# Cross-attention and gated FFN on one core: TensorE's matmuls in another order by forms of tiles

## The reference, cut to what matters

```python
q = layernorm(x) @ Wq + bq;  k = ctx @ Wk + bk;  v = ctx @ Wv + bv
scores = einsum('bhqd,bkd->bhqk', q, k) / sqrt(16)
scores = where(mask == 0, -1e9, scores)
x = x + (softmax(scores) @ v).reshape(b, s, 256) @ Wo + bo          # "x1"
xm = mix(layernorm(x))                     # three neighbouring tokens, weighted
idx = argmax(tanh(xm @ Wo1 + bo1) @ Wo2 + bo2)                      # one of nine paths
y = (xm @ W1[idx] + b1[idx]) @ W2[idx] + b2[idx]
out = x + layernorm(layernorm(x) + y) * gamma + beta
```

## Time and profile before

| | before |
|---|---|
| median of 3 runs | 337.5 us (337.3, 337.5, 338.87) |
| profiled execution | 338.19 us, its span 336.4 us |
| PE busy | 304.2 us, 90% of the span |
| DVE busy | 263.4 us, 78% |
| POOL busy | 218.2 us, 65% |
| ACT busy | 183.3 us, 54% |
| mean granted TensorE clock | 0.977 |

### The profile page before, as it was taken

One profiled execution on the slowest core, in us unless ns is written; L12 is line 12 of the kernel. 1 busy time (PEld: TensorE's weight loads), 2 busy tenths in 40 slices (PEclk: granted clock), 3 DMA queues, 4 the chain that ended last, 5 costly groups with the idle time before them and its releaser, 6 DMA issues. The chain is left out here.

```text
span 336.4 us, 7161 instructions
## 1 busy us (share of the span) xinstructions
PE 304.2 (90%) x2764; PEld 229.7 (68%) x2764; DVE 263.4 (78%) x610; ACT 183.3 (54%) x284; POOL 218.2 (65%) x259
## 2 busy tenths in 40 slices
PE   1687889699899999999999999999999999899991
PEld 1574366376567967796678767796779677876891
DVE  1776698998569796989879796989399768495876
ACT  1353906705883576727871778457653655356620
POOL 0192331892097579984996499957886598519454
PEclk9999779959999999999999999999999999999998
DMA  7932020002002001200111001000100010001003
GB/s 216 249 81 79 2 78 3 0 3 78 3 0 80 2 0 64 62 19 3 62 32 50 0 20 47 1 2 0 64 2 1 3 64 0 0 2 50 14 3 125
DMA packets 20587, 13.16 MB, mean 39 GB/s; under 512 B 10113, under 2 KB 20426, under 8 KB 20554
## 3 DMA queue, kind: packets, MB, share of 16 engines
q1 hardware_dynamic: 18914, 12.14, 12.5%
q10 hardware_dynamic: 1640, 0.57, 0.8%
HBM read 8.51 MB, written 4.19 MB: 38 GB/s over the span
## 5 line engine op out<-in xcount | busy, mean ns | idle before, releaser
L1519 POOL TENSOR_TENSOR rs<-ve,halfneg 128x4 f32<-128x4 f32 x22 | 23.6, 1072 | 49.6 <-DVE ve L1164 49.6
L905 ACT ACTIVATE e<-ps 128x1024 f32<-128x1024 f32 x32 | 31.1, 1024 | 14.1 <-PE ps L584 14.1
L1201 DVE TENSOR_REDUCE mx<-ps 128x16 f32<-128x1024 f32 x32 | 38.0, 1215 | 0.3 <-PE ps L547 0.3
L1612 POOL TENSOR_TENSOR hml<-hs,hmh 128x512 fp32r<-128x512 f32 x28 | 35.0, 1280 | 4.6 <-ACT hmh L967 4.6
L707 PE MATMUL ps<-w2h,hmh 128*128 128x256 f32 (+1 forms) x140 | 35.1, 288 | 0.0
L620 PE MATMUL ps<-wo,osb 128*128 128x256 f32 x128 | 34.1, 416 | 0.2 <-DVE osb L1228 0.2
L708 PE MATMUL ps<-w2l,hmh 128*128 128x256 f32 (+1 forms) x140 | 34.1, 280 | 0.0
L1321 DVE TENSOR_TENSOR hs<-hs,ps 128x512 f32<-128x512 f32 x28 | 18.6, 684 | 17.3 <-PE ps L687 17.3
L1577 POOL TENSOR_TENSOR y<-xh2f,gms 128x256 f32<-128x256 f32 x24 | 20.4, 882 | 16.2 <-DVE xh2f L1173 16.2
L930 ACT ACTIVATE xh<-x,vb,rs 128x256 f32<-128x256 f32 x24 | 12.5, 591 | 31.5 <-POOL vb L1532 31.5
L620 PEld LDWEIGHTS ps<-wo,osb 128*128 128x128 f32 x128 | 25.2, 206 | 5.4 <-issue 0.4
(11 more groups left out here) (174 smaller groups left out, 800.6 us busy)
## 6 DMA issues: line engine op xcount, KB each, us to landing
xin<-in_x SPq DMA_DIRECT2D x8, 512.0 KB, 3.9
out<-y SPq DMA_DIRECT2D x6, 512.0 KB, 2.9
min_<-in_mask_Bx1xSxS_ik SPq DMA_DIRECT2D x8, 128.0 KB, 3.9
hs<-in_L_ffn_W SPq DMA_DIRECT2D x2, 288.0 KB
hs<-in_L_ffn_W SPq DMA_DIRECT2D x1, 512.0 KB
out<-y SPq DMA_DIRECT2D x2, 256.0 KB, 2.1
out<-xin SPq DMA_DIRECT2D x2, 256.0 KB, 2.3
cst<-in_constants SPq DMA_DIRECT2D x1, 384.0 KB, 6.8
```

The source lines that it names most:

```text
L905: nc.scalar.activation(e[:, 2 * i:2 * i + 2, :], ps[:, bank:bank + 2, :], ACT.Exp).then_inc(s_e, 1)
L1201: v.tensor_reduce(mx[:, k, :].rearrange("p (a h) -> p a h", a=2), ps[:, bank:bank + 2, :].rearrange("p a (h s) -> p a h s", s=SK), AX.X, A ...
L1519: g.tensor_tensor(ln[7][:, :], ln[6][:, :], halfneg[:, :], ALU.pow).then_inc(s_r, 1)
L1612: g.tensor_tensor(L.lo(m, r), L.selected(m, r), L.hi(m, r).bitcast(F32), ALU.subtract).then_inc(L.s_hl, 1)
```

## The change

Three things move; no instruction is added or taken away.

1. In `scores_transposed` the groups' banks change: groups 0 and 2 take banks 2 and 3, groups 1 and 3 take 4 and 5, and the exponential writes its two groups to e with a stride. L572's matmuls go in the order 0, 2, 1, 3. The maximum's pass (32*128) goes ahead of the mask's (64*128), which is now last and carries `s_st`. The wait for `s_nT` now stands ahead of both.
2. In PE's step with an f: rep 1 and rep 2 follow each other, then the two `scores_for_max` 0 and 1; rep 3 and rep 4 follow each other, and `scores_for_max` 2 goes behind `project_out` (2, 3), beside number 3.
3. In DVE's step with an f, `take_max` 2 goes behind both `x1_stats`, beside number 3.

```diff
+        PAIR_ORDER = (0, 2, 1, 3)
+        SCORE_BANK = [2 + PAIR_ORDER.index(g) for g in range(4)]
...
+                for g in PAIR_ORDER:
+                    if t and g < 2:
+                        pe.wait_ge(s_e, at(b, NJ * 4, j * 4 + g + 1))
+                    nc.tensor.matmul(ps[:, SCORE_BANK[g], :], ksth[quarter(g), :], qr[quarter(g), t, :], start=True, stop=False)
                 for g in range(4):
-                    if t and g % 2 == 0:
-                        pe.wait_ge(s_e, at(b, NJ * 4, j * 4 + g // 2 + 1))
-                    nc.tensor.matmul(ps[:, 2 + g, :], ksth[quarter(g), :], qr[quarter(g), t, :], start=True, stop=False)
...
-                for g in (0, 2, 1, 3):
-                    r = half_rows(g // 2)
-                    nc.tensor.matmul(ps[:, 2 + g, :], mask_ident[r, 0:P], mT[r, j, :], start=False, stop=False)
                 if t == 0:
                     pe.wait_ge(s_nT, at(b, NJ, j + 1))
                 for g in range(4):
-                    nc.tensor.matmul(ps[:, 2 + g, :], max_rows[quarter(g), t * P:(t + 1) * P], nmT[quarter(g), :],
+                    nc.tensor.matmul(ps[:, SCORE_BANK[g], :], max_rows[quarter(g), t * P:(t + 1) * P], nmT[quarter(g), :],
+                                     start=False, stop=False)
+                for g in PAIR_ORDER:
+                    r = half_rows(g // 2)
+                    nc.tensor.matmul(ps[:, SCORE_BANK[g], :], mask_ident[r, 0:P], mT[r, j, :],
                                      start=False, stop=True).then_inc(s_st, 1)
...
                 if f:
                     rep(*f, 1)
+                    rep(*f, 2)
                     if front:
                         scores_for_max(*front, 0, banks)
-                    rep(*f, 2)
-                    if front:
                         scores_for_max(*front, 1, banks)
...
                     rep(*f, 3)
-                    if front:
-                        scores_for_max(*front, 2, banks)
                     rep(*f, 4)
                 if n:
                     project_out(*n, (2, 3))
                 if f and front:
+                    scores_for_max(*front, 2, banks)
                     scores_for_max(*front, 3, banks)
...
-                    bank = 2 + 2 * (i % 2)
-                    nc.scalar.activation(e[:, 2 * i:2 * i + 2, :], ps[:, bank:bank + 2, :], ACT.Exp).then_inc(s_e, 1)
+                    g = i % 2
+                    nc.scalar.activation(e[:, 4 * half + g:4 * half + g + 3:2, :], ps[:, 2 + 2 * g:4 + 2 * g, :],
+                                         ACT.Exp).then_inc(s_e, 1)
...
-                    if front:
-                        take_max(*front, 2, banks)
                     if n:
                         x1_stats(*n, 0)
                         x1_stats(*n, 1)
                     if front:
+                        take_max(*front, 2, banks)
                         take_max(*front, 3, banks)
                         split_max(*front)
```

More of the change, by code:

```diff
@@ L568, in scores_transposed @@
                     pe.wait_ge(s_mx, at(b, NJ * NT, (j + 1) * NT))
+                for g in PAIR_ORDER:
+                    if t and g < 2:
+                        pe.wait_ge(s_e, at(b, NJ * 4, j * 4 + g + 1))
+                    nc.tensor.matmul(ps[:, SCORE_BANK[g], :], ksth[quarter(g), :], qr[quarter(g), t, :], start=True, stop=False)
                 for g in range(4):
-                    if t and g % 2 == 0:
-                        pe.wait_ge(s_e, at(b, NJ * 4, j * 4 + g // 2 + 1))
-                    nc.tensor.matmul(ps[:, 2 + g, :], ksth[quarter(g), :], qr[quarter(g), t, :], start=True, stop=False)
-                for g in range(4):
-                    nc.tensor.matmul(ps[:, 2 + g, :], kstl[quarter(g), :], qr[quarter(g), t, :], start=False, stop=False)
+                    nc.tensor.matmul(ps[:, SCORE_BANK[g], :], kstl[quarter(g), :], qr[quarter(g), t, :], start=False, stop=False)
                 pe.wait_ge(s_ql, at(b, NJ * KD, j * KD + t + 1))
                 for g in range(4):
-                    nc.tensor.matmul(ps[:, 2 + g, :], ksth[quarter(g), :], ql[quarter(g), t, :], start=False, stop=False)
-                for g in (0, 2, 1, 3):
-                    r = half_rows(g // 2)
-                    nc.tensor.matmul(ps[:, 2 + g, :], mask_ident[r, 0:P], mT[r, j, :], start=False, stop=False)
+                    nc.tensor.matmul(ps[:, SCORE_BANK[g], :], ksth[quarter(g), :], ql[quarter(g), t, :], start=False, stop=False)
                 if t == 0:
```

## The result

| | before | after |
|---|---|---|
| median of 16 runs each, side by side | 337.62 us (336.14 to 340.15) | 335.67 us (334.14 to 338.67) |
| profiled execution, and its span | 338.19 us, 336.4 us | 336.16 us, 334.4 us |
| mean granted clock | 0.977 | 0.974 |

The ratio is 0.9942, 95% interval [0.9919, 0.9964]: 2.0 us faster, where 3.3 us were forecast. The time lies in the range (332.3 to 336.1), 1.5 us above the forecast of 334.2. Lines have moved by two to four: L574, L577, L584, L580 of before are now L577, L580, L584 (maxima) and L588 (mask); L543 is L545, L612 L616, L620 L624, L687 L691, L707 L711, L1217 L1220, L905 L907.

The account below looks back on a forecast made before the run. PE's order was taken as the bound between 84 and 262 us, with DVE nearly so before. Terms 2.25 + 0 + 1.05 = 3.3 us off the profiled 338.19 us, adjusted to the runs' median, gave 334.2 us, range 332.3 to 336.1.

Parts of the forecast that it names:

- A change of form costs about 0.1 us: PE's matmul passes: switching tile form costs about 0.1 us at full clock; scores were to save 0.09 us at 16 places.
- the change doesn't do what it says: Rival: the 0.1 us belongs to the two-round pass or returns in a longer first pass; 337.3 us, chance 0.09.
- the weighed rule's sum of 3.6 us: Skill's rule that tiling-mode changes drain the engine: 36 changes at 0.1 us give 3.6 us, plus what earlier exponentials bring.
- The first pair is swallowed by the wait for osb: One-hots and score tiles, first four: second tile still waits for DVE's normalised attention, so the saving is 0 us.
- Earlier exponentials: ACT starts 0.3 us earlier behind the mask's first round; with scores' savings 0.57 us in (0,0), 0.39 in (0,1) and (1,0).
- The two passes of scores give 0.09 for t = 0: Step (0,1): 0.09 us from the scores at t = 0, with 0.3 for the earlier release, makes 0.39 us.
- 0.39 us by the same sum: Step (1,0): PE's 0.91 us wait for ACT's hidden 0, behind the exponential, shortens by 0.39 us.
- DVE passes the gain on: Steps (0,0) and (0,1): DVE's reciprocal waits for PE, 1.8 us in all, so PE's earlier arrival is not lost there.
- 2 x 0.09 us each are left: Five steps (1,1) to (3,1): PE doesn't wait for the exponential, so only the scores' saving remains, 0.9 us together.
- It is cover for later and no gain: DVE's moved reduction: statistics come 1.2 us sooner, but PE's t2 doesn't wait for them in these steps; 0 us.
- the first steps keep their time: Rival: before 84 us DVE or the clock eats the gain, and rep 2's wait bites; 335.7 us, chance 0.18.
- The rival of the spared clock: Rival: the earlier exponential spares the low-clock stretch in the projection of (0,1), 1.9 us; 332.3 us, chance 0.08.

Follow-up runs that it names:

- E2: Kernel before with the new order of PE's and DVE's steps (one-hots, score tiles, reduction), its scores as they were: median 335.72 us, ratio 0.9974.
- E6: Changed kernel with rep 2 back between score tiles 0 and 1: a single run, 337.43 us.
- E3: Changed kernel with the groups in their old banks and both exponentials of a half released by the mask's last matmul: median 335.01 us, ratio 0.9936.
- E10: Changed kernel with seven useless matmuls where PE waits for DVE's inverse in (0,0) and (0,1): median 334.79 us, ratio 0.9894.
- E11: Kernel before with the same seven useless matmuls in (0,0) and (0,1), on the same chip as E10: median 336.97 us, ratio 0.9965.
- the filled pair: E10 and E11, the changed kernel and the kernel before, each with seven useless matmuls at PE's waits: 2.2 us apart by median.
- E5: Changed kernel with take_max 2 back in its old place in DVE's step, PE's order as changed: median 338.91 us, ratio 1.0017.
- E4: Changed kernel with seven useless matmuls where PE waits for DVE's inverse in (0,0) and (0,1), an earlier run: median 334.2 us, ratio 0.9908.

## Why the prediction was right, and where it was too large

The direction and the range held, and so did the sign of each part but for (0,1) and (3,1); the sum was 1.3 us too large. By its own steps:

- **A change of form costs about 0.1 us**: right. The scores give 0.10 us for each pass set (0.09 forecast), rep 3 to W2 0.22 (0.21), and E2 gives 0.20 to 0.21 us in each of four steps. The rival that the change doesn't do what it says is out. So is the weighed rule's sum of 3.6 us: E6 shows that the changes of form in the first four bring nothing where a wait stands behind them, and the rest was partly lost.
- **The first pair is swallowed by the wait for osb**: right, by E6. Rep 2's wait for ACT came, and the room behind it fell to 0.08 us in odd steps, but it doesn't bite: the second score tile stays 1.47 us behind rep 1.
- **Earlier exponentials**: the mechanism was right (the exponential of (0,0) starts at 30.73 and not 31.04, the waits are 0.99, 0.91 and 0.69 us and not 1.20, 1.12 and 0.91, and E3 takes this back). But ACT's wait of 0.27 us in (0,0), taken as a second saving, is a term that failed: that wait exists only when the scores before it fall in a low stretch. In this pair they did, and PE led by 45.92 - 45.20 = 0.72 us at the projection; then the projection, reached sooner, had more of its matmuls in the next low stretch, 4.84 us against 4.49, and the lead at the end of the step was 0.36. At the full clock (E10, E11), counted from the step's first pass, the lead is 0.30 at both places. So the low clock first gave and then took, and what (0,0) lacks of the 0.57 is that term.
- **"The two passes of scores give 0.09 for t = 0" in (0,1), and "0.39 us by the same sum" in (1,0)**: the release came, the 0.09 us did not. The product behind these scores waits for its transposed input, and PE gets there no sooner. From the first scores of t = 0 to those of t = 1 both kernels take 5.63 to 5.64 us in either step (52.36 to 57.99 in before, 52.00 to 57.64 in after), and in (1,0) of E11 and then of E10 the wait takes up what was saved, PE's timeline:

```profile
78.87 0.73 PE L449 MATMUL ps<-xTh,wqh 128*128 128x512 f32 x2 [0.69 <-DVE xTl L1195]
```

```profile
78.38 0.73 PE L451 MATMUL ps<-xTh,wqh 128*128 128x512 f32 x2 [0.78 <-DVE xTl L1198]
```

- **"DVE passes the gain on"**: this is the step that failed in (0,1). DVE's reciprocal did start 0.65 us sooner (64.16 against 64.81), but the cast behind it went from 0.32 to 0.58 us, and PE's lead fell from 0.66 to 0.39 us. The low clock took 0.20 us more, and the forecast -0.39 became +0.16; in the filled pair it is -0.05.
- **"2 x 0.09 us each are left" in (1,1) to (3,1)**: true in even steps, half true in odd ones, where the cast reaches 0.45 us and the spread starts at 135.08 and not at about 134.99, 0.55 behind the row at 134.44. In (3,1) nothing was left: PE's wait for rDs went from 0.2 to 0.4 us.
- **"It is cover for later and no gain"**: right for the difference as forecast, wrong as a reading of the change. E5 shows that without DVE's move PE's order loses 0.64 us in a middle step. I had costed DVE's move against the old place of PE's tile, and not against the new one, where DVE would stand 1.05 us waiting for it.
- **(1,0)** gave 0.49 of 0.60 us (0.54 in the filled pair). The step's order gave its 0.21 (E2); the missing 0.1 us is the 0.09 for t = 0, as told above.

The shortfall by steps in the plain pair: 0.21 us in (0,0), 0.55 in (0,1), 0.11 in (1,0), 0.21 in the four steps behind it and 0.22 from (3,1) on, which is 1.30 us, the 3.3 forecast less the 2.0 measured. In the filled pair on one chip the gain is 2.2 us, so only about 0.2 of the 1.3 is the clock's. The rest is in terms of the sum: 0.27 in (0,0) for ACT's second wait, about 0.26 in (0,1) for the cast, 0.09 each in (0,1) and (1,0) for t = 0, 0.2 in the odd steps for the cast, and 0.2 to 0.3 from (3,1) on, where the last part differs by 0.1 us and more between runs of the same code and can't be divided further. Of the rivals, "the first steps keep their time" comes nearest in time (335.7 us) and in place: (0,0) and (0,1) together gave 0.20 of 0.96 us. Its second cause, rep 2's wait, came but cost nothing.

The rival of the spared clock did not come by itself. E4 and E10, which are one kernel, show what it is worth: their medians are 1.5 and 0.9 us below the changed kernel's 335.67, measured at other times, and 3.2 and 3.6 us below that of the kernel before measured beside them. That is the fastest kernel of this study.

## What to carry to other kernels

Where one engine is the bound, read its timeline by starts and put neighbours of one tile form together: each change of form saved was 0.1 us, but only where no wait stands behind it. When an engine arrives sooner, look at what the engine that it feeds runs beside: here a lead of 0.66 us was cut to 0.39 where an operation of a third engine, for which nobody waited, was under way. A wait seen in one profile is a saving only if it would be there without the low clock: the 0.27 us of ACT's were not. And if a tile is moved on the producer, move its reader by the same distance, or the reader's queue stands still in front of it.

## What the runs showed of the hardware that I had not expected

- The low stretches of the clock (the 1.2 GHz level) came at the same times in before and after, though PE stood 0.7 us apart: a lead that runs into such a stretch is cut (4.84 against 4.49 us for the same 16 matmuls). In other runs they lay elsewhere (E3: 22.2 to 25.6 and 66.5 to 73.4 us). With seven useless matmuls in each of two waits none of five profiles had a low stretch between the first of them and the last slice (granted clock between 28 and 84 us 0.88 in after, 1.00 in E4 and E10), and the medians were 0.9 to 1.5 us shorter for the changed kernel and 0.8 to 1.4 us for the kernel before.
- A cast of 128x128 on DVE took 0.23 us alone and up to 0.85 us beside POOL's additions, ending each time 0.08 us behind the end of the POOL instruction; a product of 128x6 took 0.16 us alone and 0.22 to 0.76 us in the same way, ending 0.02 us behind it. The delay shows in no wait: the instruction itself is longer.
